# Zone tiles of a routed feed-forward stage: register reads on four engines instead of two, and two sets of sums

## The reference, cut to what matters

```python
pooled = x.mean(axis=1)
h = jnp.tanh(pooled @ W1 + b1)
logits = h @ W2 + b2
probs = jax.nn.softmax(logits, axis=-1)
top_p, top_i = jax.lax.top_k(probs, 3)
top_w = top_p / top_p.sum(axis=-1, keepdims=True)
w = jnp.einsum('bk,bke->be', top_w, one_hot(top_i, 8))
for e in range(8):
    z = gelu(x @ Wa[e]) @ Wb[e]          # 128 -> 512 -> 128
    zone_outputs = zone_outputs + z * w[:, e, None, None]
return x + zone_outputs
```

## Time and profile before

| | us |
|---|---|
| median of three executions | 3565.22 |
| lowest, highest | 3564.43, 3567.53 |
| the profiled execution, its own time | 3569.85 |
| its span, first to last instruction | 3567.4 |
| stage 3, from the memset of `acc` to the last sum (trace) | 524.64 to 920.95 |
| first up product, last down product's end | 578.15, 909.51 |

### The profile page before, as it was taken

The page is one execution under the profiler, slowest core; times in us unless marked ns, Lnnn a source line. Parts: engine busy times, 40 slices in busy tenths (PEclk is TensorE's granted clock), DMA queues, the critical chain, the costliest instruction groups (busy, mean ns, idle before and its releaser), DMA issues. The chain is left out here.

```text
span 3567.4 us, 71583 instructions
## 1 busy us (share of the span) xinstructions
PE 2775.8 (78%) x27711; PEld 1903.6 (53%) x27711; DVE 1985.0 (56%) x4314; ACT 1301.5 (36%) x2144; POOL 1374.6 (39%) x1374
## 2 busy tenths in 40 slices
PE   4987764666799997978588878777676999994294
PEld 2654443555577765557233333244444888883294
DVE  2654554111577774653289999854565666654123
ACT  3432221211111112422266666643232666561153
POOL 3644441000221215535277777743354111203655
PEclk8988886999899998979789999998687999995697
DMA  6000002333000001004200000000000000001275
GB/s 222 2 1 1 1 1 60 108 107 110 21 3 2 3 3 47 11 25 134 70 0 1 1 0 1 1 1 1 1 1 7 8 8 5 5 2 39 76 231 159
DMA packets 105822, 132.19 MB, mean 37 GB/s; under 512 B 38864, under 2 KB 84304, under 8 KB 105040
## 3 DMA queue, kind: packets, MB, share of 16 engines
q1 hardware_dynamic: 98320, 112.85, 10.6%
q0 software_dynamic: 7168, 14.78, 1.2%
HBM read 103.64 MB, written 25.35 MB: 36 GB/s over the span
## 5 line engine op out<-in xcount | busy, mean ns | idle before, releaser
L661 POOL TENSOR_SCALAR arena<-arena 128x4 f32<-128x4 f32 x120 | 27.5, 229 | 1398.6 <-DVE arena L653 1148.3
L2562 POOL TENSOR_TENSOR arena<-arena 128x512 f32<-128x512 f32 x256 | 319.1, 1270 | 141.8 <-ACT arena L2493 141.1
L2623 DVE TENSOR_TENSOR_SCAN arena<-ps,arena 128x512 f32<-128x512 f32 x256 | 311.1, 1215 | 41.4 <-ACT ps L2504 22.7
L2375 PE MATMUL ps<-arena,const_w 128*128 128x512 f32 x512 | 279.4, 629 | 12.6 <-DVE arena L2631 11.5
L163 PEld LDWEIGHTS ps<-L_attn_w,arena 128*128 128x128 f32 x1984 | 243.1, 194 | 53.0 <-issue 42.0
L163 PE MATMUL ps<-L_attn_w,arena 128*128 128x128 f32 x1984 | 259.4, 282 | 8.0 <-POOL arena L2575 3.4
L2504 ACT ACTIVATE ps<-arena,aneg 128x504 f32<-128x504 f32 x256 | 174.3, 681 | 120.1 <-DVE arena L2623 119.9
L1013 DVE SCALAR_TENSOR_TENSOR arena<-ps,arena 128x64 f32 x216 | 61.3, 284 | 280.0 <-PE ps L889 253.9
L879 PE MATMUL ps<-arena 128*128 128x256 f32 x432 | 128.3, 449 | 112.2 <-issue 107.5
L1702 PE MATMUL ps<-arena,L_attn_w 128*128 128x512 f32 x384 | 183.6, 614 | 0.9 <-ACT arena L725 0.9
L429 ACT ACTIVATE arena<-ps 128x1024 f32<-128x1024 f32 x96 | 98.3, 1024 | 217.6 <-PE ps L331 217.6
(11 more groups left out here) (446 smaller groups left out, 6598.6 us busy)
## 6 DMA issues: line engine op xcount, KB each, us to landing
arena<-zone_w SPq DMA_DIRECT2D x54, 512.0 KB
arena<-pair_w SPq DMA_DIRECT2D x40, 578.0 KB
arena<-rt SPq DMA_DIRECT2D x24, 384.0 KB
arena<-arena SPq DMA_DIRECT2D x216, 32.0 KB, 1.8
pair_in<-pair_free SPq DMA_DIRECT2D x1, 5200.0 KB, 28.7
arena<-pair_in SPq DMA_DIRECT2D x40, 130.0 KB
arena<-ctx SPq DMA_DIRECT2D x16, 256.0 KB, 3.4
arena<-pair_out SPq DMA_DIRECT2D x16, 256.0 KB, 4.9
```

The costliest lines, as they stand in the source:

```text
L2375: pe.matmul(acc(c), e.ident, hc(m, c), start=(k == 0), stop=(k == N - 1)).then_inc(s["acc_mm"], 1)
L2562: q.tensor_tensor(bu(m, c), du(g, c), bs(m), ALU.mult).then_inc(s["bu_done"], 1)
L2623: v.tensor_tensor_scan(hs(m, c), at(c), bu(m, c), 0.0, ALU.mult, ALU.add).then_inc(s["hs_done"], 1)
```

## The change

- SyncE issues sequences 0 and 1 of a tile, with both reads ahead of both transfers. ScalarE reads and issues sequence 2 on its own queue, for tile t+3 behind the GELUs of tile t. GpSimd reads the place of sequence 3 and copies it itself.
- `down` is made in two halves of 128 columns into two banks, that of sequences 2 and 3 first, and counts `down_mm` twice per tile.
- VectorE sums sequences 0 and 1. For sequences 2 and 3, ScalarE multiplies from PSUM by the weight into `staged`, and GpSimd adds that into a second set of sums, `acc2`, which has its own memset ahead of the normalisation.
- At the end each block is two products with the identity, of `acc` and `acc2`, summed in PSUM, in place of one transpose.
- The arena is widened from 20500 to 24900 floats per partition.

```diff
--- before.py
+++ after.py
@@ -33,7 +33,7 @@
 BF16 = mybir.dt.bfloat16
 STAGES = tuple(range(1, 13))
 LATE = {"L1_ffn": "L0_ffn", "L3_ffn": "L0_ffn", "L3_xattn": "L1_attn"}
-ARENA = 20500
+ARENA = 24900
 
 
 CNT = [0]
@@ -812,15 +812,17 @@
 
 
 
+
     T, U = ZT, ZT * ZU
     TOK = ZU * S
     names = PN_SEMS + ("pool_done r1_mm r1_act r2_mm lg_done ex_done cnt_mm cnt_cp q_done u_mm seq_done w_done rows_done zeroed "
                        "dve_own x_sum x_in0 x_in1 x_in2 x_in3 w_in0 w_in1 w_in2 w_in3 up_mm act_done down_mm "
-                       "acc_done z_mm")
+                       "acc_done z_mm x_cp st_done add_done")
     with block_of(nc, "zone_ffn", names) as (block, s):
         room = Room(e.arena)
         xn, hid = room.pair(GT), room.pair(FC * TOK)
         xnT_all, acc, wt_all, xT_all = room.take(NG * GT), room.take(NG * GT), room.take(4 * 2 * FC * P), room.take(4 * TOK)
+        acc2, staged = room.take(NG * GT), room.pair(2 * S)
         xnT = lambda g: xnT_all[:, g * GT:(g + 1) * GT]
         wt = lambda t: wt_all[:, (t % 4) * 2 * FC * P:(t % 4 + 1) * 2 * FC * P]
         xT = lambda t: xT_all[:, (t % 4) * TOK:(t % 4 + 1) * TOK]
@@ -844,15 +846,16 @@
                 if t < T:
                     if t >= 4:
                         sp.wait_ge(s["up_mm"], 2 * (t - 3))
-                    for u in range(ZU):
-                        first = sp.value_load(seqs[0:1, t * ZU + u:t * ZU + u + 1], min_val=0, max_val=(NS - 1) * S)
-                        sp.dma_start(xT(t)[:, u * S:(u + 1) * S], xnT_all[:, bass.ds(first, S)]
+                    first = [sp.value_load(seqs[0:1, t * ZU + u:t * ZU + u + 1], min_val=0, max_val=(NS - 1) * S)
+                             for u in range(2)]
+                    for u in range(2):
+                        sp.dma_start(xT(t)[:, u * S:(u + 1) * S], xnT_all[:, bass.ds(first[u], S)]
                                      ).then_inc(fourth("x_in", t), 16)
 
             def weights(t):
                 if t < T:
                     if t >= 4:
-                        sp.wait_ge(s["down_mm"], t - 3)
+                        sp.wait_ge(s["down_mm"], 2 * (t - 3))
                     first = sp.value_load(rows[0:1, t:t + 1], min_val=0, max_val=(E - 1) * P)
                     sp.dma_start(wt(t), e.zone_w[bass.ds(first, P), :]).then_inc(fourth("w_in", t), 16)
 
@@ -871,7 +874,8 @@
         def _(pe):
             def up(t):
                 if t < T:
-                    pe.wait_ge(fourth("x_in", t), 16 * ZU * (t // 4 + 1))
+                    pe.wait_ge(fourth("x_in", t), 16 * 3 * (t // 4 + 1))
+                    pe.wait_ge(s["x_cp"], t + 1)
                     pe.wait_ge(fourth("w_in", t), 16 * (t // 4 + 1))
                     if t >= 2:
                         pe.wait_ge(s["act_done"], 2 * (t - 1))
@@ -884,11 +888,14 @@
             def down(t):
                 pe.wait_ge(s["act_done"], 2 * (t + 1))
                 if t >= 2:
-                    pe.wait_ge(s["acc_done"], ZU * (t - 1))
-                for f in range(FC):
-                    ins = pe.matmul(e.bank(4 + t % 2)[:, 0:TOK], wt(t)[:, (FC + f) * P:(FC + f + 1) * P],
-                                    hid(t)[:, f * TOK:(f + 1) * TOK], start=(f == 0), stop=(f == FC - 1))
-                ins.then_inc(s["down_mm"], 1)
+                    pe.wait_ge(s["acc_done"], 2 * (t - 1))
+                    pe.wait_ge(s["st_done"], t - 1)
+                for h in range(2):
+                    for f in range(FC):
+                        ins = pe.matmul(e.bank(6 - 2 * h + t % 2)[:, 0:P], wt(t)[:, (FC + f) * P:(FC + f + 1) * P],
+                                        hid(t)[:, f * TOK + (1 - h) * P:f * TOK + (2 - h) * P], start=(f == 0),
+                                        stop=(f == FC - 1))
+                    ins.then_inc(s["down_mm"], 1)
 
             for g in range(NG):
                 ln.turn(pe, g)
@@ -910,8 +917,14 @@
                 down(t)
             for g in range(NG):
                 if g == 0:
-                    pe.wait_ge(s["acc_done"], ZU * T)
-                transpose_group(pe, e, e.bank(g), acc[:, g * GT:(g + 1) * GT]).then_inc(s["z_mm"], 1)
+                    pe.wait_ge(s["acc_done"], 2 * T)
+                    pe.wait_ge(s["add_done"], 2 * T)
+                for j in range(NT):
+                    k = g * NT + j
+                    pe.matmul(e.bank(g)[:, j * P:(j + 1) * P], acc[:, k * P:(k + 1) * P], e.ident, start=True, stop=False)
+                    ins = pe.matmul(e.bank(g)[:, j * P:(j + 1) * P], acc2[:, k * P:(k + 1) * P], e.ident, start=False,
+                                    stop=True)
+                ins.then_inc(s["z_mm"], 1)
 
         @block.scalar
         def _(a):
@@ -921,17 +934,60 @@
             a.activation(hr, r1, ACT.Tanh, bias=W("b1"), scale=1.0 / S).then_inc(s["r1_act"], 1)
             a.wait_ge(s["lg_done"], 1)
             a.activation(lg, lg, ACT.Exp).then_inc(s["ex_done"], 1)
+
+            def sequence(t):
+                if t < T:
+                    first = a.value_load(seqs[0:1, t * ZU + 2:t * ZU + 3], min_val=0, max_val=(NS - 1) * S)
+                    a.dma_start(xT(t)[:, 2 * S:3 * S], xnT_all[:, bass.ds(first, S)]).then_inc(fourth("x_in", t), 16)
+
+            def stage(t):
+                a.wait_ge(s["down_mm"], 2 * t + 1)
+                if t >= 2:
+                    a.wait_ge(s["add_done"], 2 * (t - 1))
+                for u in range(2):
+                    k = t * ZU + 2 + u
+                    ins = a.activation(staged(t)[:, u * S:(u + 1) * S], e.bank(6 + t % 2)[:, u * S:(u + 1) * S],
+                                       ACT.Identity, scale=wtab[:, k:k + 1])
+                ins.then_inc(s["st_done"], 1)
+
+            a.wait_ge(s["seq_done"], 1)
+            for t in range(3):
+                sequence(t)
+            a.wait_ge(s["w_done"], 1)
             for t in range(T):
                 if t >= 2:
-                    a.wait_ge(s["down_mm"], t - 1)
+                    a.wait_ge(s["down_mm"], 2 * (t - 1))
                 for h in range(2):
                     a.wait_ge(s["up_mm"], 2 * t + h + 1)
                     a.activation(hid(t)[:, 2 * h * TOK:2 * (h + 1) * TOK], e.bank(2 * (t % 2) + h),
                                  ACT.Gelu_apprx_tanh).then_inc(s["act_done"], 1)
+                sequence(t + 3)
+                if t >= 1:
+                    stage(t - 1)
+            stage(T - 1)
 
         @block.gpsimd
         def _(p_):
+            p_.memset(acc2, 0.0)
             p_.memset(acc, 0.0).then_inc(s["zeroed"], 1)
+
+            def sequence(t):
+                if t < T:
+                    first = p_.value_load(seqs[0:1, t * ZU + 3:t * ZU + 4], min_val=0, max_val=(NS - 1) * S)
+                    if t >= 4:
+                        p_.wait_ge(s["up_mm"], 2 * (t - 3))
+                    p_.tensor_copy(xT(t)[:, 3 * S:4 * S], xnT_all[:, bass.ds(first, S)]).then_inc(s["x_cp"], 1)
+
+            def summed(t):
+                first = [p_.value_load(seqs[0:1, t * ZU + 2 + u:t * ZU + 3 + u], min_val=0, max_val=(NS - 1) * S)
+                         for u in range(2)]
+                p_.wait_ge(s["st_done"], t + 1)
+                for u in range(2):
+                    if t or u:
+                        p_.wait_ge(s["add_done"], 2 * t + u)
+                    place = acc2[:, bass.ds(first[u], S)]
+                    p_.tensor_tensor(place, place, staged(t)[:, u * S:(u + 1) * S], ALU.add).then_inc(s["add_done"], 1)
+
             for g in range(NG):
                 ln.rstd(p_, g)
                 if g >= 1:
@@ -939,6 +995,13 @@
                     p_.tensor_tensor(e.X(g - 1), e.X(g - 1), xn(g - 1), ALU.add).then_inc(s["x_sum"], 1)
             p_.wait_ge(s["ln_xn"], NT * NG)
             p_.tensor_tensor(e.X(NG - 1), e.X(NG - 1), xn(NG - 1), ALU.add).then_inc(s["x_sum"], 1)
+            p_.wait_ge(s["zeroed"], 1)
+            p_.wait_ge(s["seq_done"], 1)
+            for t in range(3):
+                sequence(t)
+            for t in range(T):
+                sequence(t + 3)
+                summed(t)
 
         @block.vector
         def _(v):
@@ -1003,12 +1066,12 @@
 
             def summed(t):
                 first = [v.value_load(seqs[0:1, t * ZU + u:t * ZU + u + 1], min_val=0, max_val=(NS - 1) * S)
-                         for u in range(ZU)]
-                v.wait_ge(s["down_mm"], t + 1)
-                for u in range(ZU):
+                         for u in range(2)]
+                v.wait_ge(s["down_mm"], 2 * t + 2)
+                for u in range(2):
                     k = t * ZU + u
-                    if k:
-                        v.wait_ge(s["acc_done"], k)
+                    if t or u:
+                        v.wait_ge(s["acc_done"], 2 * t + u)
                     place = acc[:, bass.ds(first[u], S)]
                     v.scalar_tensor_tensor(out=place, in0=e.bank(4 + t % 2)[:, u * S:(u + 1) * S],
```

## The result

The changed kernel takes **3443.39 us** (median of four executions, 3436.54 to 3447.34) against 3564.94 for the kernel before on the same chip: a ratio of **0.9656**, 95% interval 0.9637 to 0.9674, 3.4% faster. The forecast was 3446.4, with a range of 3433 to 3505. The profiled execution took 3446.75 us, span 3444.8.

The account below looks back on a forecast made before the run. The prediction took SyncE's queue of reads and transfer issues as the bound. Its terms, -122.2 - 4.9 - 3.0 + 7.8 + 3.5, sum to -118.8 us, giving 3451.0 profiled and 3446.4 against the median, range 3433 to 3505.

Parts of the forecast that it names:

- The bound: Tile loop: SyncE's queue sets the pace, 6.02 us between weights, with four sequence transfers at 1.22 us each.
- The period: Tile loop: time per tile falls from a mean of 6.11 to 3.76 us, -122.2 us over 52 periods.
- the allowance of 0.1: Tile loop: 0.1 us added to SyncE's 3.67 because four queues within half a microsecond wait for each other.
- the upper level: TensorE in the loop: granted clock of 1.00 (2.4 GHz) once its idle time is gone, against 0.91 on average.
- From the last weights to the last product: End of the loop: unchanged, 0 us, as the transfer and products are the same.
- Start: Before the weights of tile 1: four sequence issues stand ahead instead of eight, -4.9 us.
- gap: Last product to transposes: about 1.0 us instead of 4.02, -3.0 us.
- end: Transposes to last sum: 128 instructions take 14.2 us plus 1.0 for the last add, +7.8 us.
- memset: Ahead of the norm: a second memset on GpSimd, fully on the path, +3.5 us.
- Dearer reads: Rival, chance 0.31: register reads on GpSimd or ScalarE cost more and bind the loop; 3483 us at 1.0 a read.
- Table swap: Rival, chance 0.04: ScalarE loads two activation tables in each tile, 6.48 us a tile, 3588 us.
- Transfers: Rival, chance 0.02: transfers bind after all, or reads still block SyncE; period stays 6.11, 3569 us.

Follow-up runs that it names:

- the two isolating kernels: The changed kernel with SyncE issuing all four sequences again, 3583.65 us; the changed kernel with all four sums on VectorE, one down product and single transposes, 3451.72 us.

## Why the prediction was right

**The bound: right.** SyncE's queue of reads and issues set the loop, and the two isolating kernels show it from both sides. The prediction set the Trainium skill's rule (DMA: Bandwidth & Descriptors, Issuing engines are not separate DMA queues) against it: several issuing engines save only sequencer time, usually little beside the transfer. Four sequences issued by one queue (period 6.16), or three by two queues and the fourth copied (3.62), agree with the first half and not with the second, since the issuing sequencer was the long part here.

**The period: the right mechanism, 0.14 too long.** SyncE alone was put at 3.67 and measured 3.62, so the allowance of 0.1 for four queues that wait for each other was the step that was off. They were not four within half a microsecond: only TensorE, at 3.51, is near. GpSimd has 2.50 where the sum gave 3.26: I counted three hops between engines (there is one in its own work, 0.18 between the adds), a read as 0.6 and none of it as hidden. ScalarE is through a tile in 2.6 and then waits 0.93 for the next up product (697.68), where I had 3.59, or 3.2 with its read hidden: the read doesn't show at all (the GELU ends at 695.57, the issue starts at 695.60), and the two evictions take 0.52 together, not 0.70. TensorE's 3.51 came out to the hundredth, and its clock went to 0.99 as the upper level assumed. This term alone is 7.0 us of the error.

**From the last weights to the last product: +1.0, predicted 0.** I had reasoned that transfer and products are the same. But TensorE follows SyncE at a distance, 3.8 to 5.7 us between the weights' issue and their up product (3.5 to 3.7 nearly always before), and that distance is open at the end (4.55 for the last tile, 3.55 before). The same numbers correct a sentence of the prediction that entered no term: weights do not leave three periods ahead of their use. Where SyncE is the bound it is one to one and a half periods, and where TensorE is, 6.1 us.

**Where the 5.9 us of waits come from.** SyncE gives weights every 3.56 us (690.84, 694.40) with a longer interval of 3.88 to 4.06 every eighth tile; before, where the mean was taken, the longer one was about every fifth. That is 24 transfers issued from one to the next against 25. TensorE at 3.51 gains on it until it meets a transfer that hasn't landed. What the pauses are no run here separates.

**Start, gap, end, memset: right** within 0.4 us each. The 14.2 us for 128 instructions came out as 0.223 for each pair of them, as the pair stage's rows say, at a granted clock of 1.00 from 785 to 800 us; the 32 transposes of before ran at 0.55.

**The rivals.** Dearer reads (0.31): a read on GpSimd is 0.54 and the rival began at 0.74; ScalarE still waits 66.8 us for the up product. What it would have looked like, the kernel with three more reads shows. Table swap (0.04): ScalarE loads one table in the loop, at 586.86, for its first GELU. Transfers (0.02): 0.60 busy.

**The total.** The forecast of 3446.4 lies 3.0 above the median, closer than the 6.4 us by which the sum missed the stage: between the two profiled executions the stages around it took 2.6 us more, less than the 11 us over which the four times of this kernel spread, and that closeness is luck.

## What to carry to other kernels

When an engine's idle time has no engine that ends it, lay out the issuing queue in the timeline and price it per transfer: a transfer whose place comes from a table cost 1.22 us of the queue that issues it, and spreading such issues over queues that wait brought 3.3% here by itself. After each bound that is removed, write down the sum of every queue again: the same second half of this change costs 10.7 us without the first and brings 12.2 with it. A fixed cost beside the loop (a memset ahead of the norm, twice the products at the end) is worth a look of its own: those two and one more copy on GpSimd hold the last 19 us of the stage.

## What the runs showed of the hardware that I had not expected

- A memset on GpSimd held up an operation of VectorE on 64x8 until the memset's end: 3.06 and 3.05 us instead of 0.16, in two kernels, and not when ScalarE wrote the zeroes. Seven other operations beside the memsets kept their times. Adds of 128x512 on both engines at once took 1.65 instead of 0.68 on VectorE, 1.60 on average instead of 1.27 on GpSimd. The Trainium skill (SBUF — State Buffer, Who interferes with whom) has VectorE and GpSimd share a pair of ports that one of them holds for a whole instruction, and says that ScalarE waits for nobody. These rows agree with it, though neither was written as a test of ports.
- The same code ahead of stage 3 reached it at 524.71, 526.46, 526.84, 529.34 and 533.15 us in different executions. It isn't the wider arena, since the kernel with GpSimd's second copy has it and began at 524.62. In the first pair the later start came with a lower clock of TensorE between 400 and 500 us (0.72 against 0.79), but the latest of all had 0.78 there; what sets it stays open.
